# Expert rows split in row layout two tiles ahead and turned by transposing DMA transfers in place of TensorE

## The reference, cut to what matters

```python
h = _layernorm(x, axis=-1) * (1 + ca) + sa
x = x + ga * _L0_attn_ref(h, W_q, W_k, W_v, W_o)         # 16 x 512 x 256
h = _layernorm(x, axis=-1) * (1 + cb) + sb
# inside x + gb * _L0_ffn_ref(h, ...): logits -> top_k (K = 2) -> softmax -> combine
for e in range(E):                                       # E = 8, D = 256, I = 1024
    h = _layernorm(hidden_states, ln_g[e], ln_b[e])
    h = gelu(jnp.einsum('bld,di->bli', h, w1[e]) + b1[e], approximate=False)
    h = jnp.einsum('bli,id->bld', h, w2[e]) + b2[e]
    out = out + combine[..., e:e + 1] * h
```

## Time and profile before

| what | us |
|---|---|
| median of 3 timed runs | 1320.15 |
| lowest, highest | 1312.46, 1320.53 |
| the profiled execution, its time | 1316.48 |
| the profiled execution, its span | 1314.7 |
| TensorE busy in the span | 1138.3 (87%) |
| VectorE, ScalarE, GpSimd busy | 937.1 (71%), 553.7 (42%), 591.4 (45%) |
| chain that ended last: TensorE's share | 68% |

### The profile page before, as it was taken

One profiled execution on the slowest core, in us unless ns is written; L12 is line 12 of the kernel. 1 busy time (PEld: TensorE's weight loads), 2 busy tenths in 40 slices (PEclk: granted clock), 3 DMA queues, 4 the chain that ended last, 5 costly groups with the idle time before them and its releaser, 6 DMA issues.

```text
span 1314.7 us, 29902 instructions
## 1 busy us (share of the span) xinstructions
PE 1138.3 (87%) x8408; PEld 894.1 (68%) x8408; DVE 937.1 (71%) x3035; ACT 553.7 (42%) x1098; POOL 591.4 (45%) x488
## 2 busy tenths in 40 slices
PE   5888787787877430999999999999999999999996
PEld 1344443443443330899999999999999999999995
DVE  5576777657777650677777777777777777777775
ACT  2565554555556220444444444444444444444442
POOL 1111454334444665344444444444444444454443
PEclk8797787677878655999999999999999999999998
DMA  5445444543434324677644475647444444444843
GB/s 165 151 145 170 160 143 171 202 153 143 159 127 168 139 79 160 208 213 215 151 86 85 85 213 146 151 85 212 87 85 86 84 86 86 85 85 88 209 85 45
DMA packets 105764, 177.38 MB, mean 135 GB/s; under 512 B 23580, under 2 KB 76968, under 8 KB 99592
## 3 DMA queue, kind: packets, MB, share of 16 engines
q1 hardware_dynamic: 71560, 120.34, 29.4%
q0 software_dynamic: 34176, 56.72, 21.7%
HBM read 228.66 MB, written 63.69 MB: 222 GB/s over the span
## 4 chain that ended last, share of the span: by engine, by line
PE 68%; DVE 10%; issue 6%; POOL 4%; ACT 2%; DMA 1%; DVEq 1%; ACTq 0%; POOLq 0%; SPq 0%
PE bank L1222 28%; PE bank L1234 28%; PE bank L1125 4%; PE bank L1211 2%; DVE st L668 2%; POOL lists L459 2%; PE bank L1187 2%; PE bank L1196 1%; PE bank L1115 1%; POOL rs L452 1%; POOL lists L502 1%; DVE resid L844 1%; DVE rowbuf L786 1%; DVE rowbuf L788 1%; ACT rowbuf L533 1%
## 5 line engine op out<-in xcount | busy, mean ns | idle before, releaser
L1222 PE MATMUL bank<-nh,wbuf 128*128 128x256 bf16 x2272 | 465.8, 273 | 2.1 <-DVE nl L979 1.5
L1234 PE MATMUL bank<-wbuf,resid 128*128 128x256 bf16 x3408 | 464.3, 273 | 0.0
L639 ACT ACTIVATE gf<-bank,b1t 128x256 f32<-128x256 f32 x568 | 268.9, 474 | 418.1 <-PE bank L1222 409.6
L495 POOL DMA_INDIRECT out<-rowbuf,ydst x142 | 227.2, 1600 | 343.8 <-DVE rowbuf L1015 290.9
L1234 PEld LDWEIGHTS bank<-wbuf,resid 128*128 128x128 bf16 x3408 | 333.5, 98 | 38.6
L1222 PE MATMUL bank<-nl,wbuf 128*128 128x256 bf16 x1136 | 310.2, 273 | 0.0
L1023 DVE CAST resid<-gf 128x256 bf16<-128x256 f32 x568 | 197.5, 348 | 154.3 <-ACT gf L639 119.6
L1025 DVE TENSOR_TENSOR resid<-gf,resid 128x256 bf16<-128x256 f32 x568 | 241.6, 425 | 19.6
L1222 PEld LDWEIGHTS bank<-nh,wbuf 128*128 128x128 bf16 x2272 | 222.7, 98 | 28.3 <-DVE nl L979 1.9
L459 POOL DMA_INDIRECT lists<-nrm,slot x128 | 138.4, 1081 | 191.6 <-DVE nrm L905 157.0
L486 POOL DMA_INDIRECT resid<-y_rows,ygb x142 | 154.8, 1090 | 64.7 <-issue 48.0
(11 more groups left out here) (187 smaller groups left out, 1132.0 us busy)
## 6 DMA issues: line engine op xcount, KB each, us to landing
wbuf<-wsplit SPq DMA_DIRECT2D x142, 1024.0 KB
rowbuf<-lists SPq DMA_DIRECT2D x71, 264.0 KB
wbuf<-in_L_ffn_w SPq DMA_DIRECT2D x16, 1024.0 KB, 6.7
wsplit<-wbuf SPq DMA_DIRECT2D x16, 1024.0 KB, 5.3
b2t<-in_L_ffn_b SPq DMA_DIRECT2D x71, 128.0 KB, 3.1
resid<-in_L_attn_x SPq DMA_DIRECT2D x16, 512.0 KB, 8.6
out<-resid SPq DMA_DIRECT2D x16, 512.0 KB, 8.0
csB<-mod_rows SPq DMA_DIRECT2D x16, 256.0 KB, 3.2
```

The costliest lines, as they stand in the source:

```text
L495: g.indirect_dma_start(out_rows, bass.IndirectOffsetOnAxis(ap=ydst[:, r, h:h + 1], axis=0), yt[:, r, h, :], None, compute_op=ALU.add).then ...
L639: a.activation(gf[:, c % 2, :], MM[c % 2][:, 0:TOK], ACT.Gelu, bias=b1t[:, r, c:c + 1]).then_inc(gf_s, 1)
L1222: last = t.matmul(MM[c % 2][:, 0:TOK], w, m[:, r, k, :], start=n == 0, stop=n == 5)
L1234: last = t.matmul(ACC[r][h][:, 0:D], g[:, c, h * P:(h + 1) * P], w, start=c == 0 and n == 0, stop=c == NI - 1 and n == 2)
```

## The change

The rows are split before they are turned. ScalarE writes the heads of `xin` into `xhl` (128 rows by 2 halves by 512 bf16: 256 heads, then 256 rests), VectorE the rests beside them. Both now do it for tile j + 2 inside tile j, at the same places (in front of chunk 5 and behind it). SyncE turns `xhl` with two `dma_start_transpose` of 128 x 512 bf16 into `nhl`, which takes the place of `nh` and `nl` (`flip`). TensorE's `turn` is gone, and `first` reads `nhl`. In SyncE's list the rows of tile j + 1 are now loaded at the head of the loads of tile j, and `flip(j)` stands between them and the table reads and weights. `rows_load` waits for `yw_s` and `nl_s`; so that a tile's rows can go early, VectorE copies their token numbers to a small tile `ytok` (one more copy of 128x2 for each tile).

```diff
             def rows_load(j, r):
-                wait_past(sp, tr_s, j - 1)
-                wait_past(sp, yt_to, j - 1)
+                wait_past(sp, nl_s, j - 1)
+                wait_past(sp, yw_s, j - 1)
...
+            def flip(j, r):
+                sp.wait_ge(nl_s, j + 1)
+                hold(sp, "sp")
+                wait_past(sp, mm1_s, NI * (j - 1))
+                hold(sp, "sp")
+                for h in range(TH):
+                    sp.dma_start_transpose(nhl[:, r, :, h * P:(h + 1) * P], xhl[:, r, h, :]).then_inc(got_nT[r], 16)
             def tile_loads(j, r):
-                rows_load(j, r)
+                if not isinstance(j, int) or j + 1 < TILES:
+                    rows_load(j + 1, 1 - r)
+                flip(j, r)
...
             rows_load(0, 0)
+            rows_load(1, 1)
             second_load(0, 0, e, new)
+            flip(0, 0)
             tile_loads(1, 1)
...
-            def head_rows(j, r):
-                act.wait_ge(tr_s, j + 1)
-                wait_past(act, mm1_s, NI * (j - 1))
-                a.activation(nh[:, r, :, :].rearrange("p k n -> p (k n)"), TR[r][:, :], ACT.Copy).then_inc(nh_s, 1)
+            def head_rows(j, half, r):
+                act.wait_ge(got_xin[r], 16 * half + 16)
+                wait_past(act, got_nT[r], 16 * TH * half)
+                hold(act, "act")
+                a.activation(xhl[:, r, :, 0:D], xin[:, r, :, 0:D], ACT.Copy).then_inc(nh_s, 1)
...
-                    if c == 5 and not last_tile:
-                        head_rows(j + 1, 1 - r)
+                    if c == 5 and not (isinstance(j, int) and j + 2 >= TILES):
+                        head_rows(j + 2, half + 1, r)
...
-                v.tensor_tensor(nl[:, r, :, :], TR[r][:, :].rearrange("p (k n) -> p k n", k=NK),
-                                nh[:, r, :, :], ALU.subtract).then_inc(nl_s, 1)
+                v.tensor_tensor(xhl[:, r, :, D:2 * D], xin[:, r, :, 0:D],
+                                xhl[:, r, :, 0:D], ALU.subtract).then_inc(nl_s, 1)
...
+                wait_past(dve, yt_to, j - 1)
+                v.tensor_copy(ytok[:, r, :], xin[:, r, :, TOKEN]).then_inc(yk_s, 1)
...
-            def turn(j, half, r):
-                for k in range(NK):
-                    for h in range(TH):
-                        last = t.transpose(TR[r][:, k * TOK + h * P:k * TOK + (h + 1) * P], xin[:, r, h, k * P:(k + 1) * P], ident[:, :])
...
-                pe.wait_ge(nl_s, j + 1)
+                pe.wait_ge(got_nT[r], 16 * TH * half + 16 * TH)
                 pe.wait_ge(got_w1[r], 16 * half + 16)
...
-                    if c == 4 and not is_last:
-                        turn(j + 1, half + r, 1 - r)
```

More of the change, by code:

```diff
@@ L138, in adaln_moe_kernel @@
         b1f = sb("b1f", [P, E, NI])
-        nh = sb("nh", [P, 2, NK, TOK], bf16)
-        nl = sb("nl", [P, 2, NK, TOK], bf16)
-        b1row = [t[:, :, :, :].bitcast(f32).rearrange("p r k n -> p (r k n)")[0:1, :] for t in (nh, nl)]
+        nhl = sb("nhl", [P, 2, 2 * NK, TOK], bf16)
+        xhl = sb("xhl", [P, 2, TH, 2 * D], bf16)
+        b1row = [t[:, :, :, :].bitcast(f32).rearrange("p r k n -> p (r k n)")[0:1, 0:512] for t in (nhl, xhl)]
         pad = sb("pad", [P, TH, RW])
-        ydst = sb("ydst", [P, 2, TH], i32); ygb = sb("ygb", [P, 2, TH], i32); yw = sb("yw", [P, 2, TH])
+        ydst = sb("ydst", [P, 2, TH], i32); ytok = sb("ytok", [P, 2, TH], i32); ygb = sb("ygb", [P, 2, TH], i32); yw = sb("yw", [P, 2, TH])
         gf = sb("gf", [P, 2, TOK])
@@ L195, in adaln_moe_kernel @@
         got_b1 = sems("got_b1"); got_b2 = sems("got_b2")
-        tr_s = sem("tr_s"); nh_s = sem("nh_s"); nl_s = sem("nl_s"); mm1_s = sem("mm1_s"); gf_s = sem("gf_s")
+        got_nT = sems("got_nT"); nh_s = sem("nh_s"); nl_s = sem("nl_s"); mm1_s = sem("mm1_s"); gf_s = sem("gf_s")
         gh_s = sem("gh_s"); gl_s = sem("gl_s"); mm2_s = sem("mm2_s"); yt_s = sem("yt_s"); y_out = sems("y_out")
-        yd_a = sem("yd_a"); yd_b = sem("yd_b"); yd_s = sem("yd_s"); yw_s = sem("yw_s"); yb_s = sem("yb_s"); yt_to = sem("yt_to")
+        yd_a = sem("yd_a"); yd_b = sem("yd_b"); yd_s = sem("yd_s"); yw_s = sem("yw_s"); yb_s = sem("yb_s"); yt_to = sem("yt_to"); yk_s = sem("yk_s")
         ohs0_s = sem("ohs0_s"); rank0_s = sem("rank0_s"); fill_s = sem("fill_s"); filli_s = sem("filli_s")
@@ L639, in gelu @@
                     a.activation(gf[:, c % 2, :], MM[c % 2][:, 0:TOK], ACT.Gelu, bias=b1t[:, r, c:c + 1]).then_inc(gf_s, 1)
-            head_rows(0, 0)
+            for r in range(2):
+                head_rows(r, 0, r)
             for j in range(2):
                 gelu(j, 0, j)
-            with a.Fori(1, TILES // 2) as h:
+            with a.Fori(1, TILES // 2 - 1) as h:
                 for r in range(2):
                     gelu(2 * h + r, h, r)
-            for j in range(TILES // 2 * 2, TILES):
-                gelu(j, j // 2, j % 2, j == TILES - 1)
+            for j in range((TILES // 2 - 1) * 2, TILES):
+                gelu(j, j // 2, j % 2)
         @block.vector
@@ L995, in targets @@
                     hold(dve, "dve")
-                v.tensor_copy(ydst[:, r, :], xin[:, r, :, TOKEN]).then_inc(yt_to, 1)
+                dve.wait_ge(yk_s, j + 1)
+                v.tensor_copy(ydst[:, r, :], ytok[:, r, :]).then_inc(yt_to, 1)
             def evacuate(j, half, r):
@@ L1031, in tile @@
                         targets(j, half, r)
-                    if c == 5 and not last_tile:
-                        split_rows(j + 1, half + r, 1 - r)
+                    if c == 5 and not (isinstance(j, int) and j + 2 >= TILES):
+                        split_rows(j + 2, half + 1, r)
                     if c == 6 and not last_tile:
@@ L1037, in _ @@
             dve.wait_ge(x2_out, 16 * NB)
-            split_rows(0, 0, 0)
+            for r in range(2):
+                split_rows(r, 0, r)
             destinations(0, 0, 0)
@@ L1220, in first @@
                     rest = wbuf[:, r, 2048 + k * I + c * P:2048 + k * I + (c + 1) * P]
-                    for w, m in ((head, nh), (head, nl), (rest, nh)):
-                        last = t.matmul(MM[c % 2][:, 0:TOK], w, m[:, r, k, :], start=n == 0, stop=n == 5)
+                    for w, m in ((head, k), (head, NK + k), (rest, k)):
+                        last = t.matmul(MM[c % 2][:, 0:TOK], w, nhl[:, r, m, :], start=n == 0, stop=n == 5)
                         n += 1
```

6 lines of the change are left out of this document (1 added, 5 removed).

## The result

The changed kernel took 1310.33 us (median of 20 runs, 1303.15 to 1320.66) against 1319.22 (20 runs) of the kernel before: ratio 0.9941, interval 0.9919 to 0.9964. It is faster by 0.6%, inside the 1% to which the prediction gave a chance of 0.16. In a second series the ratio was 0.9906 (0.9878 to 0.9935). The profiled execution took 1307.26 us, 9.2 less than that of before; the forecast was 19.6 less. The time lies in the stated range but above the forecast's own (1284 to 1305): 1309 was the figure of rival 1, and late weights, its mechanism, are what the trace shows.

A forecast was written before the change was run, and what follows sets the result against it. The prediction took TensorE's own work to bound the second stage, 526 to 1303 us. Its terms, -30.1 + 7 + 3.5 = -19.6 from 1316.5, gave 1297 us; own range 1284 to 1305, stated range 1284 to 1322.

The forecast's parts named there:

- rival 1: Tiles with new weights: long issues make weights late, costing 18 us, plus 5 at the start; 1309 us, chance 0.19.
- The gain: TensorE, second stage: removing the turning matmuls from tiles 0 to 69 saves 70 x 0.43 = 30.1 us.
- The issue: SyncE: each transposing issue taken as 0.7 us, bounds 0.33 and 1.38, putting L370 3.7 us later.
- The term of the late weights: Seven changes of expert, two tiles each: weights land late, 1 us for each change, +7 us in all, bounds 0 and 28.
- about 1 us of DMA time lost: Tiles with new weights: DMA time lost while the pair's first load waits in SyncE, counted against 3.2 us of slack.
- The packets: DMA engines: a tile's transposes make 1,024 packets, 64 per engine, taken as 1.7 us a tile.
- Rival 2: DMA engines become the bound: transposing packets cost 86 ns or more, 62 us lost at seven changes; 1355 us, chance 0.21.
- DMA share and VectorE: Ordinary tiles: DMA share near 0.6; VectorE's work rises from about 8.4 to 8.6 us, hidden in a 10.48 us tile.
- The start: Second stage's start: first transposes queue behind 1.7 MB, so the first product starts near 529.5; +3.5 us, bounds +1.5 and +7.

The follow-up runs named there:

- e_start: e_both with the transposes of tile 0 issued ahead of the second weights of tile 0; 1301.33 us, ratio 0.9838.
- e_both: The changed kernel with the table reads ahead of the row load and one 128x1024 transposing transfer per tile in place of two; 1296.41 us, ratio 0.9843.
- e_plain: The changed kernel with its two transposing transfers per tile replaced by plain ones of the same bytes in 256-byte runs (output wrong); 1295.87 us, ratio 0.9836.
- e_w1_first: The changed kernel with a tile's table reads, first weights and first bias ahead of the two transposes; 1304.29 us, ratio 0.9890.

## Why the prediction was right and wrong

**The gain, right.** Chunks start 1.31 us apart and ordinary tiles take 10.48 us. The starts of the chunks give 30.6 us for the 70 turns where 30.1 was taken, and 778.7 - 30.6 + 3.3 + 1.1 = 752.5 agrees with the 751.6 to 753.0 above.

**The issue, wrong: the step that failed.** "I take 0.7, nearer to the low end because the regular transfers are": it took 1.28. The regular transfers were no witness, since none of them was of this kind; the true value lay by the high bound of the earlier trace rows. Two of them make 1.2 us of the lateness. The gap behind them (the table reads and the setup) was 1.94 instead of 1.45, another 0.5, and the transposes' wait let them start 0.9 to 1.0 us into the tile where 0.65 was reckoned. Together: 3.5 + 1.2 + 0.5 + 0.3 = 5.5 us into the tile, which is also the measured median.

**The term of the late weights, mis-sized by 10 us.** Foreseen were 1 us for each change, 7 in all; measured were 17.1, 2.4 for each, by rival 1's mechanism and near its 18. The load of the first tile of a pair took 5.2 to 5.7 us, less than the 6.7 of the earlier trace rows, so that these tiles lost only 0.4 us on average. The second tiles lost 1.8: the first one's delay left the engines at 134 GB/s, as the windows show, and the transposes' load came on top. The prediction had a term for this ("about 1 us of DMA time lost"), sized for a load that comes 3.7 us late; it came 5.7 late. By the prediction's own sum, with 1.5 us for a tile's transposes, the loss would have to be 1.8 + 3.2 - 3.0 = 2.0 us; that is an estimate. A part was not in the sum at all: behind the longest wait the clock fell, at 1.7 us. Rival 1 came near with its total of 18, but it had put 1.1 us on each first tile and 1.5 on each second, and 5 us on the start; that its 1309 lies so close to the measured time is in part luck.

**The packets, right.** (0.376 x 16 x 1305.5 - 0.294 x 16 x 1314.7) / (148808 - 71560) = 21.6 ns, for 544 packets in each transfer. Two of them are 1088 packets, 68 for each engine, 1.5 us of DMA time for a tile; 1.7 was taken. The Trainium skill's 261 GB/s ("DMA: Bandwidth & Descriptors", latency and other measured facts; its figure for a non-contiguous middle dimension) had given 1.0; the measured price is half as much again. The same working gives 17.2 to 25.8 ns for packets of the other forms that were run, so the price depends on the form. Rival 2 is out: an issue of 1.28 us and 1.5 us of DMA time are far from an 11 us tile. (Its sum also has a term of 3 us that the prediction doesn't explain.) The 1309 ns of the Trainium skill's "VectorE: DVE Perf Modes" for one block would have made 10.5 us for the eight; by these rows they are no price of a block when one transfer turns several.

**DMA share and VectorE, about right.** The share was forecast near 0.6; it is 0.63 over five tiles, 0.77 in the window of the earlier trace rows. VectorE has 9.04 us of 11, and behind the start of the stage TensorE never waits for it.

**The start, right in size.** First row load at 520.47, first product at 529.04: 8.57 us against 5.26, so +3.3 where +3.5 was taken. The timelines of SyncE and TensorE:

```profile
520.47 1.44 SPq L360 DMA_DIRECT2D rowbuf<-lists  x2
522.21 0.33 SPq L376 DMA_DIRECT2D wbuf<-wsplit  x1
...
524.90 2.61 SPq L387 DMA_TRANSPOSE nhl<-xhl  x2
```
```profile
529.04 2.74 PE L1232 MATMUL bank<-nhl,wbuf 128*128 128x256 bf16 x12 [44.34 <-DMA nhl<-xhl]
```

But its reason was for the larger part wrong: `e_start` shows that of 3.3 us the queue ahead holds 1.2. And 1.1 us came on top in the first four chunks, where TensorE worked longer at half its clock (1.2 GHz). The prediction had said that from 526 us on every window is busy at a clock of 1.00; its own show 3.33 of 5 us and 0.61, so that the low clock at the start, and that it could last longer, was there to be seen. Windows behind the first product, first of the changed kernel, then of the kernel before:

```profile
532.00:535.00 3.00, 2.59 (x14) 1.91 (x15) 1.90 (x6) 1.19 (x3) 0.00 (x0) 0.55 0.73 91
```
```profile
529.00:532.00 3.00, 2.59 (x24) 2.33 (x25) 2.47 (x8) 1.67 (x4) 0.28 (x1) 1.00 1.02 411
```

**What stays open.** The same 1 MB load took 5.2 to 9.8 us between issue and landing; what share GpSimd's gathers and scatters have in that was not separated, though the window at 566.92 shows their queue with 77.9% of the engines. Where an earlier L370 brought nothing (`e_both`), I can't say which traffic held it up. The price of the transposes' load, 6.7 us, is the difference of two traces whose L370 stood at 5.8 and 5.5 us; it is an estimate. And the clock fell behind waits of 2.2 to 3.1 us in some tiles (3.1 in tile 4 of the changed kernel, 2.3 in tile 23 of its second profile, 2.2 in tile 35 of `e_both`), while others kept their pace of 1.31 us a chunk at a clock of 1.00 behind waits as long (2.1 in tile 65 of the changed kernel, 2.5 in tile 36 of `e_plain`, 2.7 in tile 64 of `e_w1_first`): what decides was not settled.

## What to carry to other kernels

When work moves from a busy engine to an idle queue, price its issue and not only its bytes, and look at what stands behind it in that queue: 2.6 us of issues in front of a 1 MB load, with the table reads and waits that moved behind them, took its lead from 11.1 to 5.0 us and gave back more than half of a gain of 30 us, in 14 of 71 tiles. Move what is no transfer (reads, waits for conditions long met) ahead of the new item into time the queue waits anyway, and leave the short transfers ahead of the long ones. And when the price of an issue is bounded only by rows of other kinds, let the forecast stand where a small error in it doesn't decide, or give the high end as much weight as the low.

## What was not expected of the hardware

- A transposing issue costs SyncE 1.28 us for 128 x 512 bf16 and 1.45 for 128 x 1024; a plain issue of the same 128 x 512 in runs of 256 bytes costs 0.64 (0.70 with the gap between two), against 0.33 for a transfer in long runs.
- Behind a load of 1 MB in the same queue two transposing issues took 2.5 to 4.9 us: the issue itself slows down.
- The DMA share was 1.08 in a window that moved 114 GB/s and 1.05 in one that moved 374; in the first, 72 packets of GpSimd's queue with 0.16 MB made 0.78 of it. The share says that the engines are busy, not that they are fast.
- Packets of 256 bytes cost 21.6 ns each in transposing transfers of 128 x 512, 25.8 in one of 128 x 1024, and 17.2 in plain transfers, all worked out from the share of q1.
- Behind a wait of 3.1 us for weights TensorE's granted clock was 0.66 over a window of 5 us (0.50, its lower level of 1.2 GHz, in each 1 us from 576 to 579), and two chunks took 1.0 and 0.7 us longer.
